# Three written-out middle turns of an attention stage become a hardware loop

## What is computed

```python
def _gate(x, Wsel):
    s = jax.nn.sigmoid(jnp.einsum('bsd,hed->bhse', x, Wsel))
    _, idx = jax.lax.top_k(s, K)                  # K = 2 of E = 8
    mask = jax.nn.one_hot(idx, E, dtype=s.dtype).sum(-2)
    return s * mask

q = _rope(jnp.einsum('bsd,hdp->bhsp', x, Wq))     # 16 heads of 64
k = _rope(jnp.einsum('bsd,hdp->bhsp', x, Wk))
gv = _gate(x, Wsel_v)
v = jnp.einsum('bsd,bhse,hedp->bhsp', x, gv, Wv)
att = jax.nn.softmax(jnp.einsum('bhsp,bhtp->bhst', q, k) / np.sqrt(P), axis=-1)
o = jnp.einsum('bhst,bhtp->bhsp', att, v)
go = _gate(x, Wsel_o)
return jnp.einsum('bhsp,bhse,hepd->bsd', o, go, Wo)
```

## Time and profile before

| what | value |
|---|---|
| median of 3 runs | 2614.67 us (2610.76 to 2615.86) |
| the profiled execution: its time, its span | 2610.76 us, 2609.0 us |
| TensorE busy, share of the span | 2208.3 us, 85% |
| VectorE busy | 1792.7 us, 69% |
| ScalarE, GpSimd busy | 1239.0 us, 1196.0 us |
| stage of the change, steps of the three middle turns | 675.6 us |
| instruction packets, queue 8 and queue 14 | 102 and 83 |

### The profile page before, as it was taken

How to read it: one execution, slowest core, us unless ns; L and a number is a source line. 1 busy time by engine, 2 the same in 40 slices (tenths; PEclk the granted TensorE clock), 3 DMA queues, 4 the chain that set the end, 5 groups by cost and what they waited for, 6 DMA issues and landing times. The chain is left out here.

```text
span 2609.0 us, 41157 instructions
## 1 busy us (share of the span) xinstructions
PE 2208.3 (85%) x13502; PEld 1573.0 (60%) x13502; DVE 1792.7 (69%) x3827; ACT 1239.0 (47%) x2557; POOL 1196.0 (46%) x1377
## 2 busy tenths in 40 slices
PE   6998668573999975759999999999999765799698
PEld 3666456462888853536656656665666454599555
DVE  5778657545788855756776786687676646477598
ACT  6887445212666642225444444444444332344365
POOL 5330046001899920137666666666666000022298
PEclk8999779765999997769999999999999887799699
DMA  1000043001666600012334433434333300000174
GB/s 46 3 2 3 9 91 71 6 1 39 142 153 153 141 4 18 6 63 77 81 86 87 97 88 85 95 71 101 83 77 81 73 6 1 33 1 1 35 172 100
DMA packets 62977, 161.84 MB, mean 62 GB/s; under 512 B 7563, under 2 KB 18572, under 8 KB 55001
## 3 DMA queue, kind: packets, MB, share of 16 engines
q1 hardware_dynamic: 62792, 159.50, 26.7%
HBM read 156.46 MB, written 3.01 MB: 61 GB/s over the span
## 5 line engine op out<-in xcount | busy, mean ns | idle before, releaser
L1986 PE MATMUL bank<-l2h_og,l2h_wo 128*128 128x512 f32 x512 | 262.3, 596 | 9.9 <-issue 6.8
L2088 ACT ACTIVATE l2h_pr<-twin,l2h_nmx 128x512 f32<-128x512 f32 x256 | 176.1, 688 | 171.3 <-PE bank L1975 114.8
L1077 POOL TENSOR_TENSOR l1m_hid_lo<-l1m_hid,l1m_hid_hi 128x512 fp32r<-128x512 f32 x136 | 216.7, 1613 | 63.4 <-ACT l1m_hid_hi L1056 62.7
L2080 ACT ACTIVATE l2h_prT<-bank 128x512 f32<-128x512 f32 x256 | 151.6, 592 | 192.5 <-PE bank L1975 192.5
L2233 DVE TENSOR_REDUCE l2h_nmx<-twin 128x2 f32<-128x1024 f32 x128 | 156.2, 1220 | 93.8 <-PE twin L1965 93.6
L2206 DVE TENSOR_TENSOR l2h_vg<-bank,l2h_gv 128x512 f32<-128x512 f32 x256 | 175.3, 685 | 49.4 <-POOL l2h_vs L2301 32.6
L2301 POOL TENSOR_TENSOR l2h_vs<-l2h_vg 128x256 f32<-128x256 f32 x256 | 191.7, 749 | 22.9 <-DVE l2h_vg L2206 21.9
L2218 DVE TENSOR_TENSOR l2h_og<-bank,l2h_gt 128x512 f32<-128x512 f32 x256 | 173.2, 680 | 4.5 <-PE bank L1986 2.7
L2296 POOL TENSOR_TENSOR l2h_plain<-l2h_plain,l2h_rotated 128x512 f32<-128x512 f32 x64 | 82.0, 1281 | 195.1 <-DVE l2h_rotated L2199 195.1
L1975 PE MATMUL bank<-ident,l2h_pr 128*128 128x128 f32 x1024 | 160.9, 280 | 0.0
L1975 PEld LDWEIGHTS bank<-ident,l2h_pr 128*128 128x128 f32 x1024 | 117.2, 141 | 67.4 <-issue 46.1
(11 more groups left out here) (636 smaller groups left out, 6193.0 us busy)
## 6 DMA issues: line engine op xcount, KB each, us to landing
l2h_gt<-l2m_gate_rows SPq DMA_DIRECT2D x128, 512.0 KB, 7.1
l1m_c<-l1m_weights SPq DMA_DIRECT2D x64, 512.0 KB, 6.4
l3m_c<-l3m_weights SPq DMA_DIRECT2D x32, 512.0 KB, 6.4
l0m_c<-l0m_weights SPq DMA_DIRECT2D x16, 512.0 KB, 6.8
l1m_w<-in_l1m_pairs SPq DMA_DIRECT2D x32, 192.0 KB, 6.2
l2h_fresh<-in_l2m_wqkv SPq DMA_DIRECT2D x8, 768.0 KB, 4.5
l2h_wo<-in_l2m_wo SPq DMA_DIRECT2D x8, 512.0 KB, 5.0
l0m_w<-in_l0m_pairs SPq DMA_DIRECT2D x8, 192.0 KB, 4.8
```

What stands on the lines that cost most here:

```text
L1077: nc.gpsimd.tensor_tensor(hid_lo[:, at, :], hid[:, (n + PRE) % 4, :], hid_hi[:, at, :], ALU.subtract)\
L1986: nc.tensor.matmul(ybank[:, :], wo[s][:, e, :], og[:, e % 4, :], start=(e == 0), stop=(e == E - 1))\
L2080: nc.scalar.activation(prT[:, j // 2 % 2, h, :, j % 2 * P:(j % 2 + 1) * P], tbank[:, :].rearrange("p (c q) -> p c q", c=TPB), ACT.Copy).th ...
L2088: nc.scalar.activation(pr[:, h, :], sbank[:, h, :], ACT.Exp, bias=nmx[:, k % 2, h:h + 1], accum_out=rs[:, g % 2, t, h:h + 1]).then_inc(exp ...
```

## The change

The three middle turns of `l2_moe_attention` become one body in a hardware loop of three iterations on each of the five engines. `it` is then a register value: the values waited for, the addresses of SyncE's transfers and the start of four operands of VectorE are computed from it.

```diff
-            def turns(step):
+            def turns(engine, step):
                 for k in range(LEAD):
                     step(0, k, False)
-                for it in range(TURNS - 1):
+                with engine.Fori(0, TURNS - 1) as it:
                     for k in range(LEAD, LEAD + TILES):
                         step(it, k, False)
                 for k in range(LEAD, TILES + TAIL):
...
-                        sp.dma_start(fresh[:, :], A["l2m_wqkv"][pair:pair + 1, :, :]
+                        sp.dma_start(fresh[:, :], A["l2m_wqkv"][bass.ds(pair, 1), :, :]
...
-                        sp.dma_start(wo[s][:, :, :], A["l2m_wo"][pair:pair + 1, :, :, :]
+                        sp.dma_start(wo[s][:, :, :], A["l2m_wo"][bass.ds(pair, 1), :, :, :]
...
-                        sp.dma_start(gate_rows[turn:turn + 1, :, :].rearrange("a r n -> (a r) n"), turned_gates)\
+                        sp.dma_start(gate_rows[bass.ds(turn, 1), :, :].rearrange("a r n -> (a r) n"), turned_gates)\
...
-                        rows = gate_rows[turn:turn + 1, row:row + E // 2, b * S:(b + 1) * S]
+                        rows = gate_rows[bass.ds(turn, 1), row:row + E // 2, b * S:(b + 1) * S]
...
-                    turns(step)
+                    turns(sp, step)
...
-                            out = nc.vector.tensor_copy(left[:, :, :, :, :], gates[:, :, :, turn * TH:(turn + 1) * TH, :])
+                            out = nc.vector.tensor_copy(left[:, :, :, :, :], gates[:, :, :, bass.ds(turn * TH, TH), :])
...
-                        heads, mine = slice(turn * TH + 2 * s, turn * TH + 2 * s + 2), slice(2 * s, 2 * s + 2)
+                        heads, mine = bass.ds(turn * TH + 2 * s, 2), slice(2 * s, 2 * s + 2)
                         if s == 0:
-                            nc.vector.tensor_tensor(go[:, :, :, :], gates[:, :, 1, turn * TH:(turn + 1) * TH, :], seen[:, :, 1, :, :],
+                            nc.vector.tensor_tensor(go[:, :, :, :], gates[:, :, 1, bass.ds(turn * TH, TH), :], seen[:, :, 1, :, :],
```

More of the change, by code:

```diff
@@ L2052, in _ @@
                     pe.wait_ge(go_copied, B)
-                    turns(step)
+                    turns(pe, step)
                     pe.wait_ge(read, TURNS * GROUPS * PIECES)
@@ L2141, in _ @@
                         copy_gates(0, q)
-                    turns(step)
+                    turns(act, step)
                     act.wait_ge(go_stored, TURNS * 16)
@@ L2274, in _ @@
                         take(0, g, n, False)
-                    turns(step)
+                    turns(dve, step)
                     dve.wait_ge(added, TURNS * GROUPS)
@@ L2330, in _ @@
                         gather(0, 0, n)
-                    turns(step)
+                    turns(pool, step)
         with Stage(nc, T, "l2f") as sf:
```

## The result

The changed kernel takes 2638.35 us, median of 4 runs (2633.63 to 2640.13), against 2614.51 us (2610.76 to 2615.86, 4 runs): ratio 1.0092, 95% interval 1.0078 to 1.0106, or 23.8 us slower. Its profiled execution took 2637.45 us with a span of 2635.7 us. The forecast was 2620 with a range of 2610 to 2634.

A forecast was written before the change was run, and what follows sets the result against it. TensorE's instruction order was taken to bound the middle turns. Register arithmetic 2.4, back-edges 2.8 and addresses with loop heads 0.2 us sum to 5.4 us over the median of 2614.67, giving 2620 us, range 2610 to 2634.

The forecast's parts named there:

- What bounds the kernel: In the middle turns, TensorE's instruction order sets the length: busy 6.93 us of a mean step of 7.03 us.
- (a) Register arithmetic: Computing wait counts in the looped steps costs 2.4 us, at VectorE's products that wait for two counts; bounds 0 to 38 us.
- (b) The back-edge: The branch back, taken twice, makes TensorE fetch the body's code again: 2.8 us in all, bounds 0 to 14 us.
- the fetch term: At each taken branch TensorE's code fetch takes 3.3 us, of which 1.4 us show; 2.8 us for two.
- the prediction's own sign of being wrong: Wrong if a stretch far from the edges differs by more than 1%, or an edge costs more than 5 us.
- the upper bound of 14 us: Both back-edges at 7.1 us each, if a fetch takes as long as a 512 KB transfer and nothing hides it.
- The cover of 1.9 us by L1999: At the back-edge, TensorE's products already issued hide 1.9 us of its code fetch.
- (c) Addresses: Register-computed addresses of SyncE's transfers and VectorE's moved starts stay hidden; with loop-head operations 0.2 us, without cover 9 us for transfers.
- Hidden: Rival, chance 0.18: body's code is held or TensorE's lead covers the fetch at the edges; 2615 to 2617 us.
- Faster: Rival, chance 0.10: register operations carry TensorE's waits before the transposes (L1973), saving 3.6 to 9.7 us; 2605 to 2611 us.
- Serial stalls: Rival, chance 0.12: fetches chain across engines or a second follows, registers exposed every step; 14 + 10 = 24 us, 2638 us.

The follow-up runs named there:

- the small loops: Kernel before plus TensorE-only loops of small matmuls ahead of the stage, bodies of 800 to 5,600 instructions; without traffic, branches took 0.2 us or 3.3 to 3.8 us.
- the small gate loads: Changed kernel with the two gate-row loads at the back-edge cut to an eighth of their bytes: 2629.01 us, ratio 1.0050.
- the weights went to step 16: Changed kernel with the loop's cut one step later and the 768 KB load of the next weights issued at k = 16: 2629.26 us, ratio 1.0059.
- the hint alone: Changed kernel with TensorE's fetcher told, at the head of each iteration, where the branch at the end goes: 2631.85 us, ratio 1.0065.
- the head alone: Changed kernel with the first instruction of TensorE's loop body placed on the first slot of a code packet: 2635.56 us, ratio 1.0082.

## Why the prediction was wrong

The direction was right, the size was not, and the range missed the result by 4 us.

**What bounds the kernel** held: TensorE's order sets the turn, and what stops TensorE is added in full.

**(a) Register arithmetic** was put at 2.4 us, at VectorE's products. It costs some 0.5 us a turn, 1.5 us in all, and on TensorE: with TensorE written out and VectorE in the loop the turn is 224.9 us, although VectorE has 189 operations of 40 ns at L2205 alone. The size was about right, the place wrong.

**(b) The back-edge** is the step that failed, in the fetch term, "2 x 1.4 = 2.8 us": it measured 20.7 us, and with over 5 us an edge the prediction's own sign of being wrong came true. Three things went into those 20.7 us. First, "a fetch takes between 2.6 and 3.8 us; I take 3.3". That is right for empty queues, 3.3 to 3.8 us by the small loops and 3.5 us by the small gate loads, but here the branch took 7.2 us, because the packet started only 4.3 to 4.6 us after it, while the loads of gate rows filled the DMA engines. The price was read from a store that runs in quiet queues, and the term left out what SyncE issues in the microsecond of the edge: the gate loads of step 12 were there to read, although their landing of 7.1 us isn't the mechanism: the packet had come before they landed. Second, the second fetch: the loop's head lay twenty instructions before a packet's end, and the second stop, 0.8 and 1.2 us, was gone with the head moved. I had it in a rival only. Third, the clock: an idle TensorE of 5.7 us was followed by 8.4 us at the lower level, 3.8 us of the cost, which no term of mine had; the upper bound of 14 us lacked it too. The cover of 1.9 us by L1999 was right: TensorE fell idle 1.8 us after the branch was issued.

**The rest of (b)** held. The body was not held, in line with the count of 2,700 instructions (2,684 in the trace). The other engines' fetches were hidden: 2.7 to 2.8 us on VectorE, as estimated, and on GpSimd 6.1 and 6.9, well over the 2.7 us of the estimate and the 3.7 us of idle time that were to cover it. Without TensorE's edge they cost nothing (0.9997).

The rule of the Trainium skill ("Runtime: NRT & Kernel Launch", instruction fetch mechanics), a stall at a taken branch whose target isn't in "the current 2-page window", was borne out as a stall: 7.2 us against 0.2. Its window was not: bodies of 800 and 1,600 instructions, more than two packets of 256, looped without a fetch. Its size for TensorE, 2,048 instructions, fits loosely with what the loops of small matmuls showed, a limit between 1,600 and 1,920. By its other sizes ScalarE's and GpSimd's bodies (417 and 478 instructions in the trace; the prediction had 430 and 466) would have fitted. But the trace shows GpSimd standing 6 to 7 us at each edge and ScalarE 2.4 us, and 17 packets on queue 14 in a turn instead of 7, so the measurement decides against that.

**(c) Addresses** cost nothing that shows, as predicted: they are in the run with TensorE written out too, at 0.9997.

**The rivals.** Hidden fell with the 7.2 us. Faster fell with its premise: 252 of the 255 waits of L1973 are still instructions of their own. Serial stalls gave 2638, the time that came, but not by its mechanism. Its second fetch at the end of a packet was real; its chain across the engines was not (with only TensorE as a loop the time is the same, 2637.62), nor was 0.1 us of register work in every step (0.5 us a turn, not 3.2). It agreed by luck, because edges of 10.3 us took the place of 7 us edges and 10 us of registers.

Of the 23.8 us, 20.7 are the edges and 1.5 the registers. The other 1.6 us are within the spread of the runs. In the profiles they have a place: the step k = 23, which in the third turn took 8.6 us after and 6.8 before, 1.8 us more. It is 6.8 to 7.0 us in some turns and 8.2 to 8.6 in others (9.9 once), in the kernel before and with TensorE written out as well; what makes it long stays open. The variants with a TensorE loop lie 1 to 5 us above the sum of their edges (10 us where the weights went to step 16).

## What to carry to other kernels

Rolling up a long body costs a code fetch at each taken branch, and its price is read at the place of the branch: what transfers are issued in that microsecond, how much work the engine has already been handed, and where the loop's head lies in its packet. On the engine that sets the pace, count the stop and what the clock takes afterwards. If a body of more than some 1,600 TensorE instructions must loop, give it the hint and the aligned head together (the hint alone left 17 us of the 24, the head alone 21), or put the edge where no transfer runs, at the price of what else moves with it; the other engines can loop as they are, if they have idle time there.

## What the runs showed of the hardware

- TensorE's taken branch: 0.21 us when the body is held (800 and 1,600 instructions), 3.3 to 3.8 us when not (1,920 and more) with quiet queues, 4.0 to 4.9 us with three transfers in flight, 6.4 to 7.3 us right behind two 512 KB broadcast loads (7.2 in the changed kernel), 0.36 to 0.47 us with the hint.
- The packet itself takes 0.9 to 1.8 us; what varies more is when it starts: 0.9 to 1.3 us after the branch in quiet queues, 3.2 to 4.6 us right behind the two broadcast loads. The next packet starts 3.1 to 3.5 us after the first in quiet queues and 3.3 to 4.0 behind those loads, so that a head near a packet's end pays twice: 0.6 to 1.2 us there, 1.6 to 1.8 with the small loads.
- The granted clock stayed at its upper level over idle times of TensorE of 2.0 and 2.2 us. It fell to 0.50 during one of 5.7 us and stayed there for 10.2 us, 8.4 to 8.7 of them with TensorE at work again; after one of 4.1 us it was at 0.50 for 6.8 us. With stops of 1.94 and 1.61 us close together it fell too, during the second.
- A branch can look short in the records (45 ns on GpSimd) while the engine's next instruction comes 6 to 7 us later; only TensorE's stop stood in the branch's own duration.
